# Gate block of a four-layer attention kernel: gates straight from the residual, products of rows on TensorE

## What is computed

```python
vision_proj = mean(ctx, axis=1) @ Wv.T + bv                 # one row of 256 per batch
text_proj   = x @ Wt.T + bt                                 # 512 x 256
agreement   = sum(text_proj * vision_proj, -1)              # 512
# three iterations; the last one's coupling is 2 * agreement
weighted    = softmax(2 * agreement, axis=tokens) * vision_proj      # 512 x 256
gate        = sigmoid(text_proj @ Wg_t.T + weighted @ Wg_v.T + bg)
fused       = x + gate * weighted
x           = layernorm(fused) * gamma + beta
```

## Time and profile before

| | us |
|---|---|
| median of 3 runs | 1622.87 |
| lowest, highest | 1618.45, 1623.59 |
| profiled execution, its own time | 1621.18 |
| its span in the profile | 1619.4 |
| TensorE busy (share of the span) | 1430.6 (88%) |
| VectorE busy | 875.5 (54%) |
| ScalarE busy | 721.2 (45%) |
| GpSimd busy | 262.8 (16%) |
| mean granted TensorE clock (of full speed) | 0.955 |

### The profile page before, as it was taken

The page is one execution under the profiler, slowest core; times in us unless marked ns, Lnnn a source line. Parts: engine busy times, 40 slices in busy tenths (PEclk is TensorE's granted clock), DMA queues, the critical chain, the costliest instruction groups (busy, mean ns, idle before and its releaser), DMA issues.

```text
span 1619.4 us, 24001 instructions
## 1 busy us (share of the span) xinstructions
PE 1430.6 (88%) x8176; PEld 714.0 (44%) x8204; DVE 875.5 (54%) x2135; ACT 721.2 (45%) x1185; POOL 262.8 (16%) x129
## 2 busy tenths in 40 slices
PE   5999798888999888888899988888899998989886
PEld 2336455423533654532443554553253355455334
DVE  2662664584266356567355446546636635655761
ACT  0662253355266234427446425352725632725461
POOL 1004131301100412210110213221011040313001
PEclk9999899989999989998999988988999998999899
DMA  9001304303200220530310022242031004033210
GB/s 354 1 1 28 84 2 92 69 11 111 67 1 7 39 66 1 101 69 1 124 54 1 8 53 53 46 78 48 3 122 53 1 7 104 2 72 60 39 59 13
DMA packets 44775, 85.28 MB, mean 53 GB/s; under 512 B 10464, under 2 KB 27872, under 8 KB 44384
## 3 DMA queue, kind: packets, MB, share of 16 engines
q1 hardware_dynamic: 40112, 71.07, 17.3%
q10 hardware_dynamic: 4528, 12.49, 3.7%
HBM read 43.68 MB, written 2.10 MB: 28 GB/s over the span
## 4 chain that ended last, share of the span: by engine, by line
PE 61%; DVE 18%; issue 11%; ACT 5%; DMA 3%; ACTq 2%; POOL 0%; DVEq 0%; POOLq 0%
PE ring L1264 7%; PE obank L1274 7%; PE ring L1220 7%; DVE nmax L1061 7%; PE ring L1429 6%; PE ring L1254 6%; PE ring L1241 3%; PE ring L1330 3%; PE obank L1479 3%; PE ring L1178 3%; PE ring L1420 3%; ACTq L689 2%; DMA q_all<-q_parts 2%; ACT q_all L758 2%; PE ring L1207 2%
## 5 line engine op out<-in xcount | busy, mean ns | idle before, releaser
L1061 DVE TENSOR_REDUCE nmax<-ring 128x2 f32<-128x1024 f32 (+1 forms) x192 | 218.6, 1175 | 54.1 <-PE ring L1429 36.4
L659 ACT ACTIVATE region_e<-region_d,nmin 128x512 f32<-128x512 f32 x256 | 182.7, 714 | 81.7 <-DVE nmin L914 80.0
L914 DVE CUSTOM_DVE_ANT_0 region_d<-ring,maskb 128x512 f32<-128x512 f32 x256 | 165.9, 686 | 92.7 <-issue 92.5
L771 ACT ACTIVATE region_e<-ring 128x1024 f32<-128x1024 f32 x192 | 183.4, 991 | 58.3 <-PE ring L1429 35.0
L758 ACT ACTIVATE q_all<-ring 2x1024 fp32r<-2x1024 bf16 x96 | 97.5, 1015 | 204.8 <-PE ring L1490 204.3
L585 POOL TENSOR_TENSOR nat_x<-nat_n,rows 128x1024 f32<-128x1024 f32 x16 | 37.6, 2351 | 640.3 <-DVE nat_n L959 472.8
L1420 PE MATMUL ring<-cbf 64*128 64x128 bf16 (+2 forms) x1280 | 133.6, 289 | 0.0
L1264 PE MATMUL ring<-region_q 64*128 64x512 f32 x512 | 126.9, 615 | 6.8 <-ACT region_q L648 5.4
L1057 DVE TENSOR_REDUCE nmax<-ring 128x4 f32<-128x512 f32 (+1 forms) x96 | 86.1, 911 | 79.5 <-PE ring L1420 78.7
L1274 PE MATMUL obank<-region_e,vs 128*64 128x512 f32 x512 | 124.0, 605 | 0.0
L1429 PE MATMUL ring<-k_tiles_a,q_all 64*128 64x512 f32 (+4 forms) x384 | 79.2, 454 | 24.2 <-DMA q_all<-q_parts 15.5
(11 more groups left out here) (178 smaller groups left out, 2205.5 us busy)
## 6 DMA issues: line engine op xcount, KB each, us to landing
q_all<-q_parts SPq DMA_DIRECT2D x160, 64.0 KB, 2.8
q_all<-q_parts ACTq DMA_DIRECT2D x128, 64.0 KB, 3.4
region_e<-in_w_f SPq DMA_DIRECT2D x8, 1024.0 KB, 6.0
k_tiles_a<-k_parts SPq DMA_DIRECT2D x96, 64.0 KB, 2.3
k_tiles_b<-k_parts SPq DMA_DIRECT2D x96, 64.0 KB, 2.3
wvo<-in_wv SPq DMA_DIRECT2D x5, 1024.0 KB, 5.3
wqk<-in_wq SPq DMA_DIRECT2D x4, 1024.0 KB, 9.6
wqk<-in_wk SPq DMA_DIRECT2D x4, 1024.0 KB, 11.5
```

Of the source, the lines that this page charges most:

```text
L659: ins = act.activation(e0[:, n % E0, h, :], sm0[:, n % 2, h, :], ACT.Exp, bias=nmin0[:, n, h:h + 1], scale=-1.0, accum_out=sum0[:, n, h:h ...
L771: act.activation(e16[:, n % 4, 2 * u:2 * u + 2, 0:nq], slot((a, "B", g, kt, u))[:, :, 0:nq], ACT.Exp)\
L914: ins = dve.tensor_tensor_reduce(out=sm0[:, n % 2, h, :], in0=slot(("S0", p, kt))[:, h, :], in1=maskb[:, :], scale=-1.0, scalar=3.0e38, op ...
L1061: dve.tensor_reduce(nmax[:, qt, 2 * u:2 * u + 2], slot(name)[:, :, 0:nk], AX.X, ALU.max, negate=True)\
```

## The change

The text projection is not computed any more. Ahead of the loop TensorE multiplies Wt into the gate weights (Wt.T @ Wg_t.T, four matmuls) and bt into a row (two), into `obank`; VectorE copies them over `w_l1["gt"]` and adds the row to `bg`. These two weights are loaded ahead of x, and Wt is no longer transposed on the host. `uv` also multiplies the vision vector into Wt, giving three columns that VectorE spreads over 128 (`vision`); `agree` then comes from `act_t` itself, with one single-row matmul for the bias. The gates are multiplied from `act_t` into the upper half of a bank (`D:2D`). `spread_gate` adds, with a stationary operand of 64 rows `rank_l` (row 0 the exponentials, row 32 ones) and a moving one `rank_r` (row 0: vp and u by the inverse sum, row 32: 0 and bg), the products of rows: the lower half of the bank becomes `weighted`, the upper half the sigmoid's argument. ScalarE applies Sigmoid from PSUM, VectorE multiplies and adds the residual. GpSimd writes the constant rows of `rank_l` and `rank_r` once per pass, ahead of `reset_tiles`. `V2` comes behind the gates, gets its bias from a single-row matmul, and is drained by ScalarE (Relu). X1 has two warming matmuls ahead of it where it had ten. In every norm the statistics of the first two tiles are taken one step earlier (`moments`). The list of jobs is two shorter, so two padding jobs end it.

```diff
-    jobs += [("X", 0), ("V2", 0), ("tp",), ("V2", 1), ("agree",), ("gate", 0), ("rcol",), ("gate", 1), ("ksum",)]
+    jobs += [("X", 0), ("agree",), ("gate", 0), ("gate", 1), ("V2", 0), ("V2", 1), ("ksum",)]
...
+            for n in ("t", "gt"):
+                load(w_l1[n][:, :, :], io["w1_" + n].rearrange("(t p) n -> p t n", p=P), "lt")
             load_act(0)
...
+                pool.wait_ge(*filled_by(("S0", PAIRS - 2, NT - 1), b))
+                row32 = ident[:, 32:33]
+                for out_of, n, table in ((0, S, ones[:, 0:1].broadcast_to([P, S])), (S, D, zero[:, 0:1].broadcast_to([P, D])),
+                                         (S + D, D, row("bg").squeeze(1))):
+                    pool.tensor_tensor(region_q[:, out_of:out_of + n], table, row32.broadcast_to([P, n]), ALU.mult).then_inc(rank_zeroed, 1)
...
+                act.activation(rank_l[0:1, :], slot(("agree",))[0:1, 0, :], ACT.Exp, bias=one_sum[0:1, 1:2], scale=2.0,
                                accum_out=one_sum[0:1, 2:3]).then_inc(*ends_drain(("agree",)))
                 for j in range(2):
-                    act.wait_ge(*drained_by(("gate", j), b))
-                    part = nat_n[:, 2 * j:2 * j + 2, :]
-                    act.activation(part, part, ACT.Sigmoid).then_inc(gate_ready, 1)
+                    act.wait_ge(*filled_by(("gate", j), b))
+                    act.activation(nat_n[:, 2 * j:2 * j + 2, :], slot(("gate", j))[:, :, D:2 * D], ACT.Sigmoid).then_inc(gate_ready, 1)
...
                 load_exp_ln()
+                load_exp_ln()
+                drain_v2(0)
                 rsqrt(0, -1)
+                drain_v2(1)
...
+            dve.wait_ge(gate_product, 1)
+            for t in range(DT):
+                dve.tensor_copy(w_l1["gt"][:, t, :], obank[:, t, 0:D]).then_inc(gate_weights, 1)
+            dve.tensor_tensor(row("bg").squeeze(1), obank[:, 0, D:2 * D], row("bg").squeeze(1), ALU.add).then_inc(gate_weights, 1)
...
+                link(dve.reciprocal(one_sum[0:1, 3:4], one_sum[0:1, 2:3]))
+                dve.tensor_scalar(rank_r[0:1, :], region_q[0:1, 1024:1024 + 2 * D], one_sum[0:1, 3:4], None, ALU.mult).then_inc(rank_ready, 1)
...
+                weighted(0)
+                link(fused(0))
+                weighted(1)
+                moments(0)
+                link(fused(1))
+                moments(1)
                 norm(0)
...
+            for i in range(DT):
+                for t in range(DT):
+                    pe.matmul(obank[:, i, 0:D], w_l1["t"][:, t, i * P:(i + 1) * P], w_l1["gt"][:, t, :], start=(t == 0), stop=(t == DT - 1))
+            for t in range(DT):
+                ins = pe.matmul(obank[:, 0, D:2 * D], spread[:, t, :], w_l1["gt"][:, t, :], start=(t == 0), stop=(t == DT - 1))
...
-                        keep_warm({1: 10, 2: 4, 3: 2, 4: 2}[n])
+                        keep_warm({1: 2, 2: 4, 3: 2, 4: 2}[n])
...
+                        pe.matmul(dst[:, i, 0:D], ones[0:1, :], row("bv2").squeeze(1)[0:1, :], start=True, stop=False)
...
+                            pe.matmul(dst[:, i, D:2 * D], act_t[:, t, m * P:(m + 1) * P], w_l1["gt"][:, t, :], start=(t == 0), stop=False,
+                                      skip_group_check=True)
+
+                def spread_gate(j):
+
+                    dst = slot(("gate", j))
+                    for i in range(2):
+                        m = 2 * j + i
+                        ins = pe.matmul(dst[:, i, :], rank_l[:, m * P:(m + 1) * P], rank_r[:, :], start=False, stop=True, skip_group_check=True)
```

More of the change, by code:

```diff
@@ L463, in _ @@
             load_x(0)
-            for n in ("t", "v", "gt", "gv"):
+            for n in ("v", "gv"):
                 load(w_l1[n][:, :, :], io["w1_" + n].rearrange("(t p) n -> p t n", p=P), "l1")
@@ L995, in _ @@
[L995 to L1004, removed]
+                dve.wait_ge(rank_zeroed, (b + 1) * 3)
@@ L1011, in mixed @@
[L1011 to L1025, removed]
-                mixed(1)
+                    dve.tensor_tensor(nat_y[:, part, :], slot(("gate", j))[:, :, 0:D], nat_n[:, part, :], ALU.mult)\
+                        .then_inc(*ends_drain(("gate", j)))
+                def fused(j):
+                    part = slice(2 * j, 2 * j + 2)
+                    dve.wait_ge(*drained_by(("gate", j), b))
+                    return dve.tensor_tensor(nat_y[:, part, :], nat_y[:, part, :], nat_x[:, part, :], ALU.add)
@@ L1030, in _ @@
                 dve.wait_ge(*drained_by(("ksum",), b))
+                for j in range(2):
+                    dve.wait_ge(*drained_by(("V2", j), b))
                 for t in range(NT):
@@ L1355, in _ @@
                     ins = pe.matmul(dst[:, 0, 0:D], spread[:, t, :], w_l1["gv"][:, t, :], start=(t == 0), stop=(t == DT - 1))
+                for i in range(DT):
+                    for t in range(DT):
+                        pe.matmul(dst[:, 1, i:i + 1], w_l1["t"][:, t, i * P:(i + 1) * P], spread[:, t, 0:1], start=(t == 0), stop=(t == DT - 1))
+                for t in range(DT):
+                    ins = pe.matmul(dst[:, 1, DT:DT + 1], spread[:, t, :], col("bt", t), start=(t == 0), stop=(t == DT - 1))
                 ins.then_inc(*ends_fill(("uv",)))
@@ L1360, in _ @@
                 turn(0, nat_x)
+                dst = start(("agree",))
+                pe.wait_ge(*drained_by(("uv",), b))
+                pe.matmul(dst[:, 0, :], vision[0:1, DT, :], ones[0:1, 0:1].broadcast_to([1, S]), start=True, stop=False)
+                pe.wait_ge(x_half, b * 5 + 1)
+                for t in range(DT):
+                    if t:
+                        pe.wait_ge(*drained_by(("X", 0), b))
+                    ins = pe.matmul(dst[:, 0, :], vision[:, t, :], act_t[:, t, :], start=False, stop=(t == DT - 1))
+                ins.then_inc(*ends_fill(("agree",)))
+                pe.wait_ge(gate_weights, 3)
+                gate(0)
+                gate(1)
+                pe.wait_ge(rank_ready, b + 1)
+                spread_gate(0)
+                spread_gate(1)
                 values2(0)
-                project_x(0, ("tp",), w_l1["t"], range(DT))
                 values2(1)
-                dst = start(("agree",))
-                pe.wait_ge(*drained_by(("tp",), b))
-                for t in range(DT):
-                    ins = pe.matmul(dst[:, 0, :], spread[:, t, :], tp_t[:, t, :], start=(t == 0), stop=(t == DT - 1))
-                ins.then_inc(*ends_fill(("agree",)))
-                gate(0)
-                dst = start(("rcol",))
-                pe.wait_ge(*drained_by(("agree",), b))
-                pe.wait_ge(agree_inv, b + 1)
-                for t in range(NT):
-                    ins = pe.matmul(dst[:, 0, t:t + 1], rrow[0:1, t * P:(t + 1) * P], one_sum[0:1, 3:4], start=True, stop=True)
-                ins.then_inc(*ends_fill(("rcol",)))
-                gate(1)
                 dst = start(("ksum",))
```

61 lines of the change are left out of this document (33 added, 28 removed).

## The result

| | before | changed |
|---|---|---|
| median, us (runs) | 1621.61 (1618.45 to 1623.59) | 1610.02 (1604.59 to 1612.83, 4 runs) |
| profiled execution, its own time | 1621.18 | 1604.59 |
| its span | 1619.4 | 1602.8 |
| mean granted TensorE clock | 0.955 | 0.963 |

The ratio is 0.9924 with an interval of 0.9906 to 0.9943: faster by 11.6 us. The profiled execution was also the fastest of the four; what that means for two of its stages is told under the sum.

What follows compares the result with a forecast made beforehand. TensorE was taken to bound the new gate block, where VectorE's chain had bound the old. 1621.18 - 17.2 - 1.7 + 2.6 - 1.0 + 0.5 = 1604.4, against the median 1606; stated 1605 us, range 1596 to 1614.

Steps and rivals of the forecast that it cites:

- The bound: Gate block, X0 to X1: TensorE's own queue is the bound, with VectorE's and ScalarE's value path 2.4 us earlier.
- the cover: Ahead of X1's transposes: values ready at 12.1 us after agree, TensorE free at 14.5, so 2.4 us to spare.
- Rival 1: Gate block: value path becomes the bound, held up by over 2.4 us through locks or table load; 1613 us, chance 0.16.
- TensorE's prices: uv and gate block: 19.6 us per pass, 18.16 after X0, where it cost 23.9; 17.2 us gained in four passes.
- Q2 to the first score: Stretch behind the gate block: 12.7 us per pass, 50.8 in four, 1.7 gained (bounds 5.7 gained to 1.5 lost).
- rival 4: Scores: bound by a chain starting elsewhere, stacking k behind GpSimd's k_parts, so the pass isn't shorter; 1624 us, chance 0.05.
- Setup: Ahead of the loop: six matmuls over 256 columns on TensorE delay q and k, 2.6 us lost once.
- Statistics: Norms outside the gate block: early statistics hide 0.08 us at each of 16, about 1 us gained, bounds 0 and 1.3.
- GpSimd: Seventh pair's scores: three more operations per pass may hold VectorE's L900; 0.5 us lost in four passes, bounds 0 and 5.
- End of the pass: Padding slots make the fourth V0 wait for the last F2's drain (0.70 us); VectorE's 4.15 us of issue time covers it.
- Rival 2: Q2 to the scores: clock stays at 2.4 GHz through meanO and the warming matmuls; 1597 us, chance 0.12.
- Rival 3: Gate block: clock falls to 1.2 GHz inside it, 8 us of work per pass taken as doubled; 1637 us, chance 0.05.

## Why the prediction came out right, and where it did not

**The bound.** Right. TensorE has no gap from X0 to X1, and neither VectorE nor ScalarE is later. Counted from the end of `agree`, the values took what the working gave them: the first tile of `nat_n` stands ready at 167.09 + 0.35 = 167.4 us, 11.9 behind it, where I had put 12.1. The transposes come at 171.3, so the cover was 3.9 us and not 2.4, because TensorE's side took 15.8 and not 14.5. In the kernel with 128 rows everywhere, where the matmuls are at the prices of the working, it is 169.17 - 166.78 = 2.4. Rival 1 did not occur.

**TensorE's prices: the step that failed.** I put 19.6 us per pass, 18.16 of them after X0, by prices of matmuls among their like. Measured after X0: 172.40 - 152.59 = 19.81, with 1.34 for `uv` in place of 1.46. The term that was mis-sized is the single-row and 64-row matmuls: their own time was right (0.86 and 0.43, the upper bound), but the changes into and out of them, which the sum put at nothing, cost 0.19 each, 2.05 us per pass over eleven changes; `ksum` at 1.68, where I took 1.95, and the transposes gave some of it back. So block and O0 together gained (103.44 - 87.01) - (68.52 - 63.16) = 11.1 us, not 17.2.

All stationary operands in the rows that I priced from the earlier trace rows have 128 rows and 128 columns. But other stages of the same trace of the kernel before held the price. Its chain, a q and k projection behind a product with a 64-column stationary operand, and a projection among its like, eight records over 512 columns both:

```profile
107.52 3.63 PE ring L1254 x8
150.34 3.43 PE ring L1220 x8
```

There the shape of the stationary operand changes once, from 128x64 to 128x128, and that costs 0.20 us. So the columns count as the rows do, and a look at a mixed stage would have given the missing term.

The Trainium skill has a rule that bears on this: "TensorEngine Tiling (Array Packing)", section "Key Properties", says that changing the tiling mode, unlike changing the tile, drains TensorE. It gives no figure. The runs agree in that such a change costs time, 0.19 us; that a drain is what takes it, no run here shows.

**Q2 to the first score.** I took 50.8 for four passes. The eight profiles of the changed kernel and its variants give 49.74 to 52.19, with a mean of 50.9; the two with the old block give 52.49 and 52.58. A gain of 1.6 us was right in size, though single passes of either kind overlap (11.9 to 13.5 against 12.6 to 13.5). The place was right too. Windows over Q2's own matmuls, the longest and the shortest of the kernel before, then the first of the changed one:

```profile
960.54:965.37 4.83, 4.83 (x9) 2.13 (x10) 0.66 (x1) 0.61 (x1) 0.00 (x0) 0.73 0.02 3
1355.58:1359.16 3.58, 3.58 (x8) 1.67 (x9) 0.66 (x1) 0.61 (x1) 0.00 (x0) 0.98 0.02 5
```

```profile
173.25:176.79 3.54, 3.54 (x9) 1.63 (x10) 0.66 (x1) 0.61 (x1) 0.00 (x0) 1.00 0.02 5
```

With the new block Q2 takes 3.54 us in all 32 passes of the eight profiles; with the old one 3.58 to 4.83 in eight passes, 4.45 in the mean. Taking warming matmuls out of the old kernel or putting them into the new one changed neither, so what is left is the wait of 4.31 us ahead of X1, which the new block does not have. That this wait is the cause is argued, not shown by a run of its own. Part of the 0.9 us was lost again behind Q2: the one-column matmuls of `meanV` take 2.44 to 4.03 us, by the clock, and in the short passes (11.9 to 12.3 us) the first score waits for the copies of q, 6.7 to 7.1 us after the first of them is issued:

```profile
185.42 0.30 PEld L1470 LDWEIGHTS ring<-k_tiles_a,q_all 64*128 64x128 f32 x4 [0.58 <-DMA q_all<-q_parts]
```

It waits for q and not for k, so rival 4 did not occur.

**Setup.** Right for the matmuls, 2.6 us. Timeline of the changed kernel on TensorE, the product of the weights (L1210, L1212) and the next V0:

```profile
32.06 1.89 PE L1210 MATMUL obank<-w_gt,w_t 128*128 128x256 f32 x8
33.78 1.03 PE L1212 MATMUL obank<-w_gt,spread 128*128 128x256 f32 x4
34.65 3.60 PE L1196 MATMUL ring<-wvo,ctx_t 128*128 128x512 f32 x8
```

34.65 - 32.06 = 2.59 us. The net loss is less in the mean: the first q projection starts at 38.08 here, and at 36.53 to 37.95 in the seven other profiles with the product, against 35.44 and 35.26 without it, 2.0 us later in the mean. From there to the first O0 it is 96.28 or 96.29 us in all ten. What gave some of it back ahead of the loop is not shown.

**Statistics.** I put 1.0, with bounds of 0 and 1.3; measured 1.9, outside of them. The step was sized by one gap of 0.09 us per norm; the transposes that no longer wait for tiles gain up to 0.2 at a norm.

**GpSimd.** The lock showed, and cost nothing. Timeline of the changed kernel at the seventh pair's scores, to be read with the 0.29 us of L900 in the earlier trace rows (it is L922 now):

```profile
115.80 1.04 POOL L589 TENSOR_TENSOR region_q<-ones,ident 128x512 f32<-128x512 f32 x1 [86.02 <-PE ring L1291]
116.41 0.58 DVE L922 TENSOR_TENSOR vs<-region_b,rs 128x128 f32<-128x128 f32 x1
```

VectorE took twice as long in the operation that met GpSimd, once in each pass; the other 124 of its kind took 0.29. But from the first q projection to the first O0, a stretch that holds this place, the kernel before takes 96.28 us as well: VectorE's slack hid it. I had charged 0.5. The Trainium skill, "SBUF — State Buffer", section "SBUF: two separate sides", has the rule of the shared port that the prediction weighed; the row fits a lock, and the 2 us by which I had put the sum worse by it did not come.

**End of the pass.** The padding slots make the fourth V0 wait for the drain of the last F2, as predicted. Timeline of the changed kernel, end of the first pass:

```profile
423.14 3.70 PE L1196 MATMUL ring<-wvo,ctx_t 128*128 128x512 f32 x8 [0.78 <-DVE nat_y L1154]
```

They are hidden in the main: the turn of a pass takes 132.17 us against 132.0 to 132.5 before. But the cover is spent, since the chain now runs from that drain over V0 to the scores. In the kernel without the early statistics, whose other norms take what they took before, the three turns cost 397.10, 0.3 to 0.5 more than with the old block (396.62 and 396.74).

**Clock.** Rival 2, a full clock through the mean output, did not occur (0.75 to 0.88). Rival 3 occurred in small, in two passes of 32: see the last section.

**The sum**, of block and O0, Q2, start, statistics and turn of the pass: -11.1 - 1.6 + 2.0 - 1.9 + 0.4 = -12.2 us, beside 11.6 and 13.5 between the medians of the two timings. The prediction stated 1605, the medians are 1610.02 and 1608.29. They lie inside 1596 to 1614 because the range had room on that side for rival 1, which did not occur; that it also covered an unpriced change of operands is luck. The first profile, 1604.59, is 5.4 us under its own median; against the second profile of the same kernel (1608.11), three short Q2 stages put it 2.45 us ahead and a short last attention in all four passes 2.9, while a slower start put it 1.55 behind. Read alone, it would have hidden the failed term behind a lucky execution. Whether the new block has a share in the 2 us or so by which the last attention is shorter in the mean of the eight profiles (293.1, against 294.9 and 296.0) stays open; one pass of it swings by 2.5.

## What to carry to other kernels

Price a matmul by what stands beside it: put matmuls whose stationary operands have the same shape together, or give a bias row 128 rows by way of a column of the identity, which took the same 0.43 and 0.86 us here. Take prices from a stage that mixes shapes as the new code will. Once an engine's queue is the bound, the next gain is in filling its last gap with work that depends on nothing near, and the number to watch is the cover of the path that was the bound before. Read one stage that repeats exactly, in several profiles, rather than the time of one execution.

## What the runs showed of the hardware

**A change of row count of the stationary operand costs TensorE 0.19 us**, between 128 and 1 rows as between 128 or 1 and 64 (0.194, 0.195 and 0.186 per change in three kernels). A change from 64 to 128 columns costs as much (3.63 against 3.43 us in the kernel before). What TensorE does in that time no run shows.

**The clock can fall inside the dense block.** In the kernel with V2's bias over 128 rows, first pass, the body of `agree` in the chain:

```profile
153.17 3.31 PE ring L1409 x4
```

A window around it (length, busy PE, PEld, DVE, ACT, POOL, clock):

```profile
153.00:156.00 3.00, 3.00 (x5) 1.30 (x5) 0.00 (x0) 0.24 (x1) 3.00 (x2) 0.59 0.00 0
```

Four records take 3.31 us instead of 1.91, at a granted clock of 0.59, and of 0.50, the lower of the two levels, from 153.54 to 156.95; the pass lost 22.08 - 20.39 = 1.7 us. The kernel with ten warming matmuls lost as much in its first pass (25.18 against 23.48), with 0.50 from 152.74 to 156.15. The other three passes of both, and every pass of the six other profiles with the new block, kept the full rate there, with the same work ahead of it, so it is an event of single passes and not a price of the block; what sets it off is not shown. It is the mechanism of rival 3, at 1.7 us once in place of 8 per pass.
